# Moving the shifted taps of two channel pairs from VectorE to TensorE in a selective-scan block

## The chip, the cores and the metric

The kernel runs on one core of a Trainium2 chip. A core has five engines, each with a queue of its own that is worked in order: TensorE (PE: matrix products and transposes, into PSUM), VectorE (DVE), ScalarE (ACT), GpSimd (POOL) and SyncE (SP, which here only issues DMAs). They meet through semaphores. The metric is the device time of one execution in microseconds.

## The reference

Two sequences of 2048 rows of 512 channels go through an adaptive layer norm, a Mamba mixer with a residual, a second adaptive norm and a mixing product with a residual. All is float32. What the change touches, cut short:

```python
h = layernorm(x) * (1 + ca) + sa
h, gate = split(h @ in_proj.T)                       # 1024 channels each
h = silu(causal_conv(h, conv_w, K=4) + conv_b)       # depthwise, 4 taps
dt, B, C = split(h @ x_proj.T)                       # 128, 16, 16
dt = softplus(dt @ dt_proj.T + dt_b)
dA = exp(dt[..., None] * A)                          # 16 states per channel
dBu = (dt * h)[..., None] * B
s_t = s_(t-1) * dA_t + dBu_t
y = sum_n(s * C) + h * D
x = x + ga * ((y * silu(gate)) @ out_proj.T)
x = x + gb * (mix(layernorm(x) * (1 + cb) + sb))     # 8 factors, summed beforehand
```

## The kernel before

The rows are cut into 16 chunks of 256 (8 for each sequence). The 1024 channels are 8 tiles of 128, taken as 4 *pairs* q = 0 to 3. A *unit* is one pair with one of the 16 states: one 128x512 operation (two tiles of 256 rows side by side). A chunk has 64 units; two units are a *step* s (32 in a chunk), four units a *quad* g (16 in a chunk, four to a pair).

For each unit ScalarE makes the decay exp(dt A) in one of three PSUM banks (`decays`), VectorE scans it with `ub` = u B (`scan`), and the state is multiplied with C. VectorE does that product for most units itself (`multiply_c`, into a ring of four `sc_d`); for the others its scan writes to `state_p`, and GpSimd multiplies one or two units of a quad at once (`multiply_c` of GpSimd, into slots of `sc_p`). How many of a quad's four units are GpSimd's is in the tables `FIRST_POOL` (chunk 0), `FOLD_POOL` (chunk 1) and `EVERY_POOL` (from chunk 2): the last ones of the quad, or the first ones where the quad closes its pair (g = 3, 7, 11, 15). TensorE sums over the states by transposing each product into `y_bank` (`turn_on_dve`, `turn_on_pool`). GpSimd also makes u = dt h (`make_u`) and ub for a quad at a time (`make_ub`, two quads ahead), and the small operations that carry the state over a chunk's border (`carry_seam`, `add_column`; ScalarE's `make_column`, `add_seam`).

Beside this inner loop, chunk c's steps hold the front part of chunk c + 1 (norm, input projection, convolution, SiLU, dt, B, C) and the back part of chunk c - 1 (gate, output projection, residual, second norm, mixing). Every engine has this order written out by hand in its `one_round(c, par, la, lc)`: a call stands under the step s (or quad g) in which it is issued. There is no planner; tables such as `IN_AT`, `TAP_AT`, `ADD_AT`, `SILU_AT` give steps for the four pairs or eight tiles, the first of two entries for chunk 0, the second for the later chunks.

The convolution of pair q goes so. TensorE projects (`project_h`, in the steps of `IN_AT`) into a PSUM bank. ScalarE's `copy_h` (`TAP_AT`) copies the bank to `pre` in SBUF with three rows of the chunk before ahead of it, and scales the bank by the unshifted tap and adds the bias. VectorE's `taps` (`TAP_AT`) adds the first shifted tap to the bank, one 128x256 operation for each of the two tiles. TensorE's `add_tap` (`ADD_AT`) adds the other two as products with diagonal matrices `tap_diag`, which GpSimd made at the start. Then come ScalarE's tanh (`tanh_before`, `SILU_AT`) and VectorE's `silu_before`, which writes `hc`. For chunk 0 VectorE does all shifted taps. In `taps` the wait stands ahead of the loop:

```python
dve.wait_ge(pre_made, PAIRS * c + q + 1)
for k in range(dve_taps(c)):
```

Within one step VectorE's order is: first scan, statistics or shifts, second scan, its C products, `silu_gate`, `gate_sums`, `residual_mixer`, `silu_before`, `taps`. A norm takes variance and mean on VectorE (`stats`, `means`), the power on GpSimd (`deviations`, two operations), and -mean/deviation on VectorE (`shifts`, one 128x1 operation for each of the two row tiles).

`U_PAIRS` is the ring of u (three pairs), `DT_PAIRS` that of dt (five). `slot_table` hands out the four slots of `sc_p` in the order of the table, and `quad_before` gives the last quad that used one of a quad's slots; GpSimd's product waits until TensorE has turned it, VectorE's scan until GpSimd has multiplied it.

Of the kernel before, what the change touches and what calls it, by code (L numbers as in the profile page):

```python
# [22 lines left out]
ALU = mybir.AluOpType  # L23
ACT = mybir.ActivationFunctionType

P = 128
# [17 lines left out]
DVE_TAPS = 1  # L44
PE_TAPS = range(DVE_TAPS, TAPS - 1)
# [3 lines left out]
IN_AT = ((2, 3, 4, 5, 7, 8, 9, 10), (1, 3, 4, 5, 8, 9, 10, 11))  # L49
TAP_AT = ({5: 0, 7: 1, 10: 2, 12: 3}, {5: 0, 7: 1, 11: 2, 13: 3})  # L50
# [3 lines left out]
U_PAIRS = 3  # L54
H_TILES, Z_TILES = 3, 3
DT_PAIRS = 5
EVERY_POOL = (2, 2, 1, 1, 2, 2, 1, 2, 2, 2, 2, 1, 2, 2, 1, 1)
# [14 lines left out]
NORMS = 2 + LB  # L72
# [15 lines left out]
def dve_taps(c):  # L88
    return DVE_TAPS if c else TAPS - 1


def tap_start(c, q):

    return 2 * (PAIRS * c + q) * DVE_TAPS + 2 * (TAPS - 1 - DVE_TAPS) * (PAIRS if c else q)
# [98 lines left out]
def build(nc, x, win_m, xp_t, dt_t, wo_t, chan, cond_t, wmod, factors, bias, out):  # L193
# [11 lines left out]
    with ExitStack() as ctx:  # L205
# [19 lines left out]
        tap_diag = sb("tap_diag", [P, len(PE_TAPS), KE, P])  # L225
        decay_rate = sb("decay_rate", [P, KE, N])
# [316 lines left out]
        def _(pool):  # L543
# [26 lines left out]
            def make_u(c, q):  # L570

                pair, k = PAIRS * c + q, slice(2 * q, 2 * q + 2)
                pool.wait_ge(dt_made, pair + 1)
                pool.tensor_tensor(u[:, pair % U_PAIRS, :, :], dt[:, pair % DT_PAIRS, :, :], hc[:, k, :], ALU.mult).then_inc(u_made, 1)  # L574
# [86 lines left out]
            def make_diagonals():  # L661
# [3 lines left out]
                for i, k in enumerate(PE_TAPS):  # L665
                    pool.tensor_tensor(tap_diag[:, i, :, :], ident[:, :].unsqueeze(1).to_broadcast([P, KE, P]),
                                       conv[:, :, k:k + 1].to_broadcast([P, KE, P]), ALU.mult).then_inc(diag_made, 1)

# [5 lines left out]
            def one_round(c, par, la, lc):  # L674
                for g in range(QUADS):
# [15 lines left out]
                    if c % PER and g == 6:  # L691
                        add_column(c, slice(2, 4), 5)
                    multiply_c(quad)
                    if g in (0, 2, 3):
                        make_u(c, max(g, 1))
# [12 lines left out]
                    if la is not None and g == 12:  # L708
# [3 lines left out]
                    if c % PER and g == 4:  # L712
# [13 lines left out]
        def _(act):  # L726
# [254 lines left out]
            def one_round(c, par, la, lc):  # L981
                for s in range(STEPS):
# [34 lines left out]
                    if c % PER and s == 12:  # L1017
                        make_column(c, 3)
                    if lc is not None and s in (1, 3, 5):
                        tanh_gate(c - 1, {1: 1, 3: 2, 5: 3}[s])  # L1020
                    if s in (4, 6, 12):
                        skip(c, {4: 1, 6: 2, 12: 3}[s])
                    if la is not None:
# [8 lines left out]
                        if s == 22:  # L1032
# [38 lines left out]
        def _(pe):  # L1071
# [74 lines left out]
            def add_tap(c, q):  # L1146

                if c == 1 and q == 0:
                    pe.wait_ge(diag_made, len(PE_TAPS))
                pe.wait_ge(tap_done, tap_start(c, q) + 2 * DVE_TAPS)  # L1150
                for j in range(2):
                    for i, k in enumerate(PE_TAPS):
# [690 lines left out]
```

## Time and profile before

| | us |
|---|---|
| median of 3 runs | 1929.47 |
| lowest, highest | 1928.4, 1930.35 |
| the profiled execution | 1929.0 |
| its span (first to last instruction) | 1927.3 |
| busy in it: TensorE, VectorE, ScalarE, GpSimd | 1720.6, 1801.3, 1546.2, 1794.0 |
| mean granted TensorE clock, share of full speed | 0.975 |

Busy time is the time in which an engine has at least one instruction under way. Times in the rows below count from the start of the span. The profile was taken in an execution of its own, whose time stands in the table beside its span.

### The profile page before, as it was taken

The page shows a single profiled execution, that of the slowest core. Times are in us where ns is not written, and L with a number is a line of the kernel's source. Part 1 is how long each engine was busy: PE and PEld are TensorE (multiplying, and loading weights), DVE is VectorE, ACT ScalarE, POOL GpSimd, SP SyncE. Part 2 cuts the span into 40 slices and gives each one's busy share as a digit, 9 for nine tenths or more (in the row PEclk, how much of TensorE's full clock was granted, in tenths as well). Part 3 has the DMA queues.
Part 4 walks back from the last instruction along what each step waited for, and adds up shares of the span by engine and source line. Part 5 has one row for each costly group of instructions (what it writes and reads, how often), then busy time and mean ns, then how long its engine had stood idle before and what let it go on. Part 6 is the DMA issues. An engine that isn't in the chain of part 4 may idle for free. (4 is left out here: it accounts for less than half of the span.)

```text
span 1927.3 us, 29502 instructions
## 1 busy us (share of the span) xinstructions
PE 1720.6 (89%) x9176; PEld 1311.1 (68%) x9176; DVE 1801.3 (93%) x2260; ACT 1546.2 (80%) x4529; POOL 1794.0 (93%) x756
## 2 busy tenths in 40 slices
PE   7995998989899998998989899998989989899798
PEld 4664767667576766767677676766768676676664
DVE  3897999999999999999999999999999999999995
ACT  3776789798888979888787988879788897988773
POOL 1899999999999999999999999999999999999993
PEclk9897999999999999999999999999999999999899
DMA  5756514032140412304042340503213041321310
GB/s 179 258 115 157 145 51 163 24 128 82 55 143 20 152 50 100 110 23 164 23 153 66 116 148 23 165 23 137 72 72 127 34 152 35 104 78 44 111 28 33
DMA packets 72077, 186.17 MB, mean 97 GB/s; under 512 B 6896, under 2 KB 8560, under 8 KB 63984
## 3 DMA queue, kind: packets, MB, share of 16 engines
q1 hardware_dynamic: 68224, 176.94, 27.1%
q0 software_dynamic: 3696, 7.34, 2.4%
q8 instruction: 73, 1.20, 0.3%
q14 instruction: 84, 0.69, 0.1%
HBM read 172.20 MB, written 12.06 MB: 96 GB/s over the span
## 5 line engine op out<-in xcount | busy, mean ns | idle before, releaser
L604 POOL TENSOR_TENSOR ub<-u,b_all 128x2048 f32<-128x2048 f32 x255 | 1166.8, 4576 | 40.7 <-DMA b_all<-bc_scratch 40.7
L756 ACT ACTIVATE decay<-dt,decay_rate 128x256 f32<-128x256 f32 x2048 | 883.7, 465 | 20.4 <-DVE state_p L1548 1.1
L1548 DVE TENSOR_TENSOR_SCAN decay<-decay,ub 128x512 f32<-128x512 f32 x617 | 729.1, 1212 | 21.7 <-ACT decay L756 16.1
L620 POOL TENSOR_TENSOR sc_p<-state_p,c_all 128x1024 f32<-128x1024 f32 (+1 forms) x256 | 499.8, 1952 | 53.1 <-PE y_bank L1088 31.6
L1548 DVE TENSOR_TENSOR_SCAN state_p<-decay,ub 128x512 f32<-128x512 f32 x407 | 480.1, 1207 | 34.5 <-ACT decay L756 32.1
L1088 PE MATMUL y_bank<-ident,sc_d 128*128 128x128 f32 x2468 | 364.6, 279 | 103.6 <-DVE sc_d L1563 103.5
L1088 PEld LDWEIGHTS y_bank<-ident,sc_d 128*128 128x128 f32 x2468 | 289.0, 143 | 180.8 <-DVE sc_d L1563 127.4
L1563 DVE TENSOR_TENSOR sc_d<-decay,c_all 128x512 f32<-128x512 f32 x617 | 395.5, 675 | 7.4 <-PE y_bank L1088 1.7
L742 ACT ACTIVATE carry<-decay 128x2 f32<-128x2 f32 x617 | 99.8, 162 | 220.4 <-DVE sc_d L1563 219.0
L1170 PE MATMUL bank_a<-hT,win_h 128*128 128x256 f32 x992 | 236.3, 384 | 15.3 <-DVE hc L1612 7.8
L1088 PEld LDWEIGHTS y_bank<-ident,sc_p 128*128 128x128 f32 x1628 | 195.6, 145 | 65.5 <-issue 33.2
L1142 PE MATMUL bank_c<-hT,win_z 128*128 128x256 f32 x960 | 235.0, 392 | 1.9
L1088 PE MATMUL y_bank<-ident,sc_p 128*128 128x128 f32 x1628 | 219.4, 280 | 19.2 <-POOL sc_p L620 19.2
L1242 PE MATMUL bank_c<-wo,yg 128*128 128x512 f32 x480 | 221.4, 594 | 0.0
L1170 PEld LDWEIGHTS bank_a<-hT,win_h 128*128 128x128 f32 x992 | 181.9, 192 | 41.0 <-DVE hc L1612 10.4
L1142 PEld LDWEIGHTS bank_c<-hT,win_z 128*128 128x128 f32 x960 | 180.5, 196 | 27.3 <-DVE xc L1661 5.3
L1242 PEld LDWEIGHTS bank_c<-wo,yg 128*128 128x128 f32 x480 | 86.8, 191 | 73.5 <-issue 72.0
L1153 PE MATMUL bank_a<-pre_z,tap_diag 128*128 128x256 f32 x480 | 119.2, 392 | 13.7 <-DVE bank_a L1603 13.7
L1153 PEld LDWEIGHTS bank_a<-pre_z,tap_diag 128*128 128x128 f32 x480 | 91.1, 195 | 41.3 <-DVE bank_a L1603 17.3
L1286 PE MATMUL bank_c<-ffn,hT 128*128 128x512 f32 x240 | 112.9, 592 | 0.0
L574 POOL TENSOR_TENSOR u<-dt,hc 128x512 f32<-128x512 f32 x63 | 84.1, 1336 | 0.0
L857 ACT ACTIVATE y_rows<-y_bank 128x512 f32<-128x512 f32 x64 | 37.3, 582 | 56.7 <-PE y_bank L1088 49.8
(137 smaller groups left out, 1813.3 us busy)
## 6 DMA issues: line engine op xcount, KB each, us to landing
win_h<-win_m SPq DMA_DIRECT2D x128, 256.0 KB, 2.6
win_z<-win_m SPq DMA_DIRECT2D x128, 256.0 KB, 2.7
b_all<-bc_scratch SPq DMA_DIRECT2D x31, 1024.0 KB, 4.7
c_all<-bc_scratch SPq DMA_DIRECT2D x31, 1024.0 KB, 5.1
xa<-x SPq DMA_DIRECT2D x16, 512.0 KB, 5.1
xc<-x SPq DMA_DIRECT2D x16, 512.0 KB, 3.8
out<-xc SPq DMA_DIRECT2D x15, 512.0 KB, 3.7
ffn<-factors POOLq DMA_DIRECT2D x7, 1024.0 KB, 10.1
```

What stands on the lines that cost most here:

```text
L604: pool.tensor_tensor(ub[:, slot, :, :, :], u[:, (PAIRS * c + q) % U_PAIRS, :, :].unsqueeze(1).to_broadcast([P, QUAD, 2, ROWS]), b_all[:, n ...
L620: pool.tensor_tensor(sc_p[:, slot:slot + k, :, :], state_p[:, slot:slot + k, :, :], c_all[:, n:n + k, :].unsqueeze(2).to_broadcast([P, k, ...
L742: act.activation(dst, src, ACT.Copy).then_inc(carried, 1)
L756: last = act.activation(bk[:, j * ROWS:(j + 1) * ROWS], dt[:, pair % DT_PAIRS, j, :], ACT.Exp, scale=decay_rate[:, e, n:n + 1])
L1088: last = pe.matmul(y_bank[:, at:at + P], tile[:, j, t * P:(t + 1) * P], ident[:, :], start=False, stop=last_of_pair, is_transpose=True, sk ...
L1142: last = pe.matmul(dst[:, j * ROWS:(j + 1) * ROWS], tile[:, k, :], hTc[:, k, :], start=(k == 0), stop=(k == KD - 1))
L1153: last = pe.matmul(h_lane(c, q)[:, j * ROWS:(j + 1) * ROWS], tap_diag[:, i, 2 * q + j, :], pre[q % 2][:, j, k:k + ROWS], start=False, stop ...
L1170: last = pe.matmul(h_lane(c, q)[:, j * ROWS:(j + 1) * ROWS], win_h[i % H_TILES][:, k, :], hT[c % H_RING][:, k, :], start=(k == 0 and j == ...
L1242: last = pe.matmul(bank_c[t][:, :], yg[:, k, t * P:(t + 1) * P], wo[:, k, :], start=(k == 0), stop=(k == KE - 1))
L1286: last = pe.matmul(bank_c[t][:, :], hT[c % H_RING][:, k, t * P:(t + 1) * P], ffn[:, k, :], start=False, stop=(k == KD - 1), skip_group_che ...
L1548: dve.tensor_tensor_scan(dst, bk[:, :], ub[:, quad % UB_RING, i, :, :].rearrange("p j r -> p (j r)"), 0.0, ALU.mult, ALU.add).then_inc(sca ...
L1563: dve.tensor_tensor(sc_d[:, i % D_RING, :, :], bk[:, :].rearrange("p (j r) -> p j r", j=2), c_all[:, n:n + 1, :].to_broadcast([P, 2, ROWS] ...
```

## The change

For chunks from 1 on, VectorE adds no tap for pairs 0 and 1; TensorE adds all three shifted taps of these pairs, with a third diagonal for their four tiles that GpSimd makes at the start. Its `add_tap` waits for ScalarE's copy there and no longer for VectorE. The ring of u has two pairs, so `make_u` waits until the pair before the last has all its ub. One 128x2 operation makes both shifts of a norm. In `EVERY_POOL` quad 0 gives GpSimd one unit instead of two, quad 3 two instead of one. And steps are moved, on all engines but SyncE:

```diff
+T3 = 2
-IN_AT = ((2, 3, 4, 5, 7, 8, 9, 10), (1, 3, 4, 5, 8, 9, 10, 11))
-TAP_AT = ({5: 0, 7: 1, 10: 2, 12: 3}, {5: 0, 7: 1, 11: 2, 13: 3})
+IN_AT = ((2, 3, 4, 5, 7, 8, 9, 10), (1, 2, 3, 4, 8, 9, 10, 11))
+TAP_AT = ({5: 0, 7: 1, 10: 2, 12: 3}, {6: 0, 7: 1, 11: 2, 13: 3})
-U_PAIRS = 3
+U_PAIRS = 2
-EVERY_POOL = (2, 2, 1, 1, 2, 2, 1, 2, 2, 2, 2, 1, 2, 2, 1, 1)
+EVERY_POOL = (1, 2, 1, 2, 2, 2, 1, 2, 2, 2, 2, 1, 2, 2, 1, 1)
-NORMS = 2 + LB
+NORMS = 3
-def dve_taps(c):
-    return DVE_TAPS if c else TAPS - 1
+def dve_taps(c, q):
+    if c == 0:
+        return TAPS - 1
+    return 0 if q < T3 else DVE_TAPS
...
 # GpSimd
+                if pair >= U_PAIRS:
+                    pool.wait_ge(ub_made, N // QUAD * (pair - U_PAIRS + 1) - 1)
+                pool.tensor_tensor(first_diag[:, :, :], ident[:, :].unsqueeze(1).to_broadcast([P, 2 * T3, P]),
+                                   conv[:, 0:2 * T3, 0:1].to_broadcast([P, 2 * T3, P]), ALU.mult).then_inc(diag_made, 1)
+                    if g == 5:
+                        make_u(c, 3)
                     multiply_c(quad)
-                    if g in (0, 2, 3):
-                        make_u(c, max(g, 1))
+                    if g in (0, 3):
+                        make_u(c, {0: 1, 3: 2}[g])
-                    if la is not None and g == 12:
+                    if la is not None and g == 11:
                         make_u(c + 1, 0)
-                    if c % PER and g == 4:
+                    if c % PER and g == 5:
                         carry_seam(c, 1)
...
 # ScalarE
-                    if c % PER and s == 12:
+                    if c % PER and s == 14:
                         make_column(c, 3)
-                    if lc is not None and s in (1, 3, 5):
-                        tanh_gate(c - 1, {1: 1, 3: 2, 5: 3}[s])
-                    if s in (4, 6, 12):
-                        skip(c, {4: 1, 6: 2, 12: 3}[s])
+                    if lc is not None and s in (1, 3, 6):
+                        tanh_gate(c - 1, {1: 1, 3: 2, 6: 3}[s])
+                    if s in (3, 6, 14):
+                        skip(c, {3: 1, 6: 2, 14: 3}[s])
-                        if s == 22:
+                        if s == 23:
                             copy_bc(c + 1)
...
 # TensorE
-                pe.wait_ge(tap_done, tap_start(c, q) + 2 * DVE_TAPS)
+                if q < T3:
+                    pe.wait_ge(pre_made, PAIRS * c + q + 1)
+                else:
+                    pe.wait_ge(tap_done, tap_start(c, q) + 2 * DVE_TAPS)
                 for j in range(2):
+                    if q < T3:
+                        pe.matmul(h_lane(c, q)[:, j * ROWS:(j + 1) * ROWS], first_diag[:, 2 * q + j, :],
+                                  pre[q % 2][:, j, 0:ROWS], start=False, stop=False, skip_group_check=True)
-                    if lc is not None and s == 25:
+                    if lc is not None and s == 26:
                         ffn_bias(c - 1, 1)
                         project_ffn(c - 1, 1, (0,))
+                        if s == 25:
+                            expand_dt(c + 1, 2)
                         if s == 26:
-                            expand_dt(c + 1, 2)
-                        if s == 27:
                             expand_dt(c + 1, 3)
-                        for q, at in enumerate((9, 10, 11, 12)):
+                        for q, at in enumerate((9, 11, 11, 12)):
-                        for q, at in enumerate((13, 15, 15, 15)):
+                        for q, at in enumerate((13, 14, 15, 15)):
...
 # VectorE
-                for t in range(LB):
-                    dve.tensor_scalar(nrm[:, 1, t:t + 1], mv[:, t, 0:1], nrm[:, 0, t:t + 1], -1.0,
-                                      ALU.mult, ALU.mult).then_inc(normed, 1)
+                dve.scalar_tensor_tensor(out=nrm[:, 1, :], in0=mv[:, :, 0], scalar=-1.0, in1=nrm[:, 0, :],
+                                         op0=ALU.mult, op1=ALU.mult).then_inc(normed, 1)
-                for k in range(dve_taps(c)):
+                for k in range(dve_taps(c, q)):
-                        if s in (1, 3, 5):
-                            silu_gate(c - 1, {1: 1, 3: 2, 5: 3}[s])
+                        if s in (1, 3, 6):
+                            silu_gate(c - 1, {1: 1, 3: 2, 6: 3}[s])
-                        if s in (15, 17):
+                        if s in (14, 17):
                             residual_mixer(c - 1, s // 17)
```

## Rows read from the trace of the kernel before

**Rows 1.** The page's busy time, share of the span and instructions of each engine.

```profile
PE 1720.6 (89%) x9176; PEld 1311.1 (68%) x9176; DVE 1801.3 (93%) x2260; ACT 1546.2 (80%) x4529; POOL 1794.0 (93%) x756
```

**Rows 2.** Timeline of VectorE: start, length, line, operation, times, [idle before, ended by].

```profile
272.46 1.22 DVE L1548 TENSOR_TENSOR_SCAN state_p<-decay,ub 128x512 f32<-128x512 f32 x1 [0.32 <-POOL sc_p L620]
...
308.47 2.34 DVE L1548 TENSOR_TENSOR_SCAN decay<-decay,ub 128x512 f32<-128x512 f32 x2
...
879.12 2.34 DVE L1548 TENSOR_TENSOR_SCAN decay<-decay,ub 128x512 f32<-128x512 f32 x2
```

**Rows 3.** Busy time in two windows: length, engines (x), clock, DMA share, GB/s.

```profile
234.00:351.00 117.00, 105.12 (x576) 80.67 (x575) 113.22 (x142) 96.64 (x287) 116.84 (x51) 1.00 0.28 96
...
879.15:993.30 114.15, 104.60 (x583) 81.01 (x582) 111.32 (x140) 95.15 (x278) 110.70 (x45) 1.00 0.28 91
```

**Rows 4.** Waits in chunk 7: who waited for whom, us in total, times, longest.

```profile
PE y_bank L1088 <- DVE sc_d L1563: 5.5, 6, 1.6
...
POOL sc_p L620 <- PE y_bank L1088: 2.3, 2, 1.6
...
DVE state_p L1548 <- ACT decay L756: 1.5, 2, 1.2
...
POOL sc_p L620 <- DVE state_p L1548: 0.9, 1, 0.9
...
DVE decay L1548 <- ACT decay L756: 0.7, 1, 0.7
```

**Rows 5.** Timeline of VectorE: the end of chunk 6, then chunk 7.

```profile
856.68 1.22 DVE L1548 TENSOR_TENSOR_SCAN state_p<-decay,ub 128x512 f32<-128x512 f32 x1 [1.25 <-ACT decay L756]
...
861.38 2.33 DVE L1548 TENSOR_TENSOR_SCAN state_p<-decay,ub 128x512 f32<-128x512 f32 x2
...
870.33 1.22 DVE L1548 TENSOR_TENSOR_SCAN state_p<-decay,ub 128x512 f32<-128x512 f32 x1 [0.65 <-ACT decay L756]
...
887.35 1.23 DVE L1548 TENSOR_TENSOR_SCAN decay<-decay,ub 128x512 f32<-128x512 f32 x1 [0.75 <-ACT decay L756]
...
895.93 1.22 DVE L1548 TENSOR_TENSOR_SCAN decay<-decay,ub 128x512 f32<-128x512 f32 x1
...
899.35 0.87 DVE L1603 SCALAR_TENSOR_TENSOR bank_a<-pre_z,conv,bank_a 128x256 f32<-128x256 f32 x2
900.27 1.22 DVE L1548 TENSOR_TENSOR_SCAN state_p<-decay,ub 128x512 f32<-128x512 f32 x1
...
903.36 1.28 DVE L1644 TENSOR_TENSOR yg<-bank_c,yg 128x512 f32<-128x512 f32 x2
...
908.58 0.87 DVE L1603 SCALAR_TENSOR_TENSOR bank_a<-pre_z,conv,bank_a 128x256 f32<-128x256 f32 x2
909.36 2.34 DVE L1548 TENSOR_TENSOR_SCAN decay<-decay,ub 128x512 f32<-128x512 f32 x2
```

**Rows 6.** Timeline of ScalarE in chunks 6 and 7.

```profile
840.19 0.17 ACT L742 ACTIVATE carry<-decay 128x2 f32<-128x2 f32 x1 [0.60 <-DVE sc_d L1563]
...
852.83 1.57 ACT L878 ACTIVATE dt<-bank_a,ch 128x256 f32<-128x256 f32 x4
...
898.15 0.99 ACT L817 ACTIVATE bank_a<-bank_a,conv 128x256 f32<-128x256 f32 x2
```

**Rows 7.** Timeline of TensorE in chunk 7 (a float32 product is two instructions).

```profile
902.73 1.89 PE L1153 MATMUL bank_a<-pre_z,tap_diag 128*128 128x256 f32 x8
904.46 1.03 PE L1088 MATMUL y_bank<-ident,sc_p 128*128 128x128 f32 x8
...
913.53 3.72 PE L1170 MATMUL bank_a<-hT,win_h 128*128 128x256 f32 x16 [0.71 <-DVE hc L1612]
...
938.26 5.32 PE L1242 MATMUL bank_c<-wo,yg 128*128 128x512 f32 x12
```

**Rows 8.** GpSimd: its timeline in chunk 6; the page's costliest group.

```profile
860.29 1.29 POOL L574 TENSOR_TENSOR u<-dt,hc 128x512 f32<-128x512 f32 x1
...
L604 POOL TENSOR_TENSOR ub<-u,b_all 128x2048 f32<-128x2048 f32 x255 | 1166.8, 4576 | 40.7 <-DMA b_all<-bc_scratch 40.7
```

More of the change, by code:

```diff
@@ L85, in parts @@
     return unit // N, unit % N
-def dve_taps(c):
-    return DVE_TAPS if c else TAPS - 1
+def dve_taps(c, q):
+    if c == 0:
+        return TAPS - 1
+    return 0 if q < T3 else DVE_TAPS
 def tap_start(c, q):
-    return 2 * (PAIRS * c + q) * DVE_TAPS + 2 * (TAPS - 1 - DVE_TAPS) * (PAIRS if c else q)
+    return 2 * sum(dve_taps(i // PAIRS, i % PAIRS) for i in range(PAIRS * c + q))
 def quad_of(unit):
@@ L225, in build @@
         tap_diag = sb("tap_diag", [P, len(PE_TAPS), KE, P])
+        first_diag = sb("first_diag", [P, 2 * T3, P])
         decay_rate = sb("decay_rate", [P, KE, N])
@@ L1148, in add_tap @@
                 if c == 1 and q == 0:
-                    pe.wait_ge(diag_made, len(PE_TAPS))
-                pe.wait_ge(tap_done, tap_start(c, q) + 2 * DVE_TAPS)
+                    pe.wait_ge(diag_made, len(PE_TAPS) + 1)
+                if q < T3:
+                    pe.wait_ge(pre_made, PAIRS * c + q + 1)
+                else:
+                    pe.wait_ge(tap_done, tap_start(c, q) + 2 * DVE_TAPS)
                 for j in range(2):
+                    if q < T3:
+                        pe.matmul(h_lane(c, q)[:, j * ROWS:(j + 1) * ROWS], first_diag[:, 2 * q + j, :],
+                                  pre[q % 2][:, j, 0:ROWS], start=False, stop=False, skip_group_check=True)
                     for i, k in enumerate(PE_TAPS):
```

## The prediction

> **What bounds the kernel now.** The page's line of busy times [rows 1] says that two engines are full: VectorE 1801.3 us and GpSimd 1794.0 of 1927.3. A share of busy time doesn't say which of them sets the pace, so I cut out single chunks. VectorE's first scan of chunk 2 begins at 308.47, that of chunk 7 at 879.12 [rows 2]: (879.12 - 308.47)/5 = 114.13 us a chunk, and chunks 2 to 14 are thirteen of this kind. In chunk 7 VectorE has 111.3 us of work in 114.15, GpSimd 110.7, TensorE 104.6, ScalarE 95.2 [rows 3]. What each waits for decides [rows 4]. VectorE waits only for ScalarE's decays: 1.5 + 0.7 us. GpSimd waits 2.3 us for TensorE (slots of its products come free when TensorE has turned them) and 0.9 for VectorE. So in these chunks GpSimd follows, and has about 3.2 us to give; VectorE with its short waits for ScalarE sets the end, and TensorE is the third part of the chain: it waits 5.5 us for VectorE's products, but from 913.53 to beyond 938.26 + 5.32 its rows follow one another without a gap [rows 7].
>
> Chunks 0 and 1 are different. From 234 to 351 GpSimd is busy 116.84 of 117 us [rows 3], and in chunk 1 VectorE's scan at 272.46 waits for it [rows 2]. A saving on VectorE before that instant is lost there, so I count no gain before chunk 2. Chunk 15 prepares no next chunk and has no taps.
>
> **The change, part by part,** in the frame of chunk 7 (step 0 at 879.12).
>
> *The taps.* For pairs 0 and 1 VectorE no longer runs two 128x256 taps each: the step that held the first pair was 900.27 - 899.35 = 0.92 us longer, the second 909.36 - 908.58 = 0.78 [rows 5]. That is 1.70 us off VectorE. TensorE gets two more matmuls a pair. Each shows as two instructions; eight take 904.46 - 902.73 = 1.73 us [rows 7], so four more are 0.87 a pair, 1.73 a chunk.
>
> *The C product that moves.* The pool takes one unit fewer in quad 0 and one more in quad 3. VectorE's product of unit 2 is added in step 1 (0.59 from start to start, by the 0.6 that each of two takes at 903.36), and that of unit 13 goes from step 6, which had 903.36 - 900.27 = 3.09 us up to the gate products and keeps two scans, 2.25: minus 0.84. In step 2 the second scan, at 887.35, waits 0.75 us for a decay that ScalarE makes after a copy and a modulation [rows 5]; ScalarE's chain to it doesn't change, so the added 0.59 fills this wait and costs nothing. Were the wait gone it would cost 0.59.
>
> So VectorE alone would be 1.70 + 0.84 = 2.54 us earlier at step 8. Three things take part of it back.
>
> (a) ScalarE's copy for the skip of pair 1 moves from step 4 to 3, ahead of the decays of step 4, which come just in time: about 0.15, between 0 and the copy's own 0.9.
>
> (b) The gate product of pair 1 in step 6 needs TensorE's transposes that ended at 902.73. VectorE now reaches it at 895.93 + 0.15 + 2.83 (step 5 without gate and tap) + 2.25 + 0.58 + 0.6 = 902.34. TensorE, in an unbroken row since the first projection of step 1, gets the product of unit 2 earlier, 0.32 after the modulation that it waits for, and saves 0.44 in step 4: 902.6. Wait: 0.3.
>
> (c) TensorE then has 0.87 more at the head of steps 6 and 8. From 902.6: six matmuls for pair 0 (2.60), the pool's products of quad 1 (0.87), transposes (0.44), one VectorE product (0.44), transposes (0.44), six matmuls of pair 1 (2.60), three pool products (1.3), one VectorE product (0.44) end at 911.75. There it starts the projection that began at 913.53 [rows 7] after waiting 0.71 for VectorE's SiLU, now done at 911.45. So TensorE is 1.78 us earlier, VectorE 2.08.
>
> From there to step 17 TensorE's work is the same and gapless, so it stays 1.78 earlier. The first half of the mixer residual moves to step 14 and needs the projection of step 12: VectorE waits about 0.5 for it, and has it out of step 15. At step 17 the second half needs the 12 matmuls that ended near 943.58, the last link that held VectorE before (a gap of 0.2). I get 1.66 us there.
>
> *Steps 18 to 31.* ScalarE makes the soft-plus of the next chunk in steps 25 and 29; VectorE waits 1.25 and 0.65 us there [rows 5], and ScalarE, once past 840.19, ran without a wait for VectorE to the first [rows 6]. These waits move with the chunk and stay. The norm's shift, two instructions of 128x1, becomes one: 0.1 us saved, twice a chunk, both ahead of these waits. I take 0; if the waits were gone it is 0.2. The later copy of B and C (step 23) gives its store one step less; but the load behind it on SyncE waits for ub products that GpSimd makes after that, so nothing comes of it. The copy also feeds the second dt expansion of step 22, which may wait for it: bounds 0 and 0.4, ahead of a wait of TensorE for VectorE; I take 0. The other two expansions and a feed-forward matmul swap places around TensorE's wait for ScalarE's y copy; same work up to the last of it, 0. Input projections one step earlier: their weights' loads wait for the first projection, still in step 1, land in 2.6 us (median of the page) and are used in step 4; 0.
>
> *GpSimd.* Its work is the same. The ring of two makes it wait only for products that its own queue has already issued. New places to wait: the product of quad 3 now reuses quad 1's slots, turned in TensorE's step 6, behind the longer taps (0.85 by the chain in (c)); the carry column of pair 3 comes in step 14; u of the next chunk, which ran at 860.29 [rows 8], stands one quad and one ub product earlier, about when dt's first half is ready, near 853.6 (852.83 + half of 1.57, [rows 6]); and quad 13 must wait for quad 12 to be turned. Behind u there wait the ub product of quad 14 and the pool product of quad 12, and behind that VectorE's scan in step 27, with a slack of 861.38 - 860.29 = 1.1 us [rows 5, 8] that u's 1.29 uses up. I get a GpSimd chunk of 110.9 + 0.85 + 0.75 = 112.5, as short as VectorE's 114.15 - 1.66 = 112.5, and set 0.15 aside for that scan. The one new diagonal product, made once, lies in GpSimd's first wait of 40.7 us [rows 8].
>
> **Sum.** 1.66 - 0.15 = 1.5 us a chunk, 13 chunks: 19.5. The profiled execution took 1929.0 us (span 1927.3): 1929.0 - 19.5 = 1909.5. The median of the runs is 0.5 above it; I say 1910.
>
> A rule of the Trainium skill (Perfetto Trace Analysis, Identifying the Most-Contended Engine) says that matmul busy time misjudges TensorE and that its headroom is read from the share of weight loads. By the rows that share is 81.0 of 114.15 us, 71%; by the rule TensorE would be far from full, (c) would fall away, and the sum would be rival 1's. The rows from 913.53 on show no gap, so I side with them.
>
> **Rivals.**
> 1. TensorE's row of matmuls doesn't hold and GpSimd keeps up: 2.54 - 0.15 = 2.4 a chunk, 31 us: 1898. For it: TensorE waited 5.5 us a chunk for VectorE. Against: the gapless stretch, and GpSimd, which has 110.7 us of work against 111.75. 13%.
> 2. GpSimd becomes the bound. Its 3.2 us of waiting a chunk shrink only if the new waits stay under 1.6; with all four paid, 0.85 + 0.4 + 0.75 + 0.25 and 0.2 to 0.8 more, a chunk is 113.4 to 114.0. Gain 2 to 10 us, 1919 to 1927. For it: 97% busy, no wait of its own from quad 8 to quad 3. Against: its waits are for TensorE and shrink when it is late. 27%, 8 of them within 0.2%.
> 3. Slower: ScalarE's copy of pair 0 comes late. It moves from step 5 to the end of step 6, behind a tanh and two skip copies; there wait TensorE's taps and, though it has no tap left, VectorE's queue (the wait for the copy stands ahead of the empty loop), with every scan behind it. The old copy ended near 899.1, VectorE got to it at 899.35 [rows 5, 6]. New: decays of unit 13 after the scan of unit 11 (898.35) end at 899.45, tanh 0.5, skip 0.85, copy 1.7: 902.4, against TensorE at 902.6 and VectorE at 903.3. From 904.4 on the gain is gone. Were it a whole step later (3.57 us: 906.0), TensorE's projection would begin at 915.1 instead of 913.53, 1.6 us a chunk, 21 us: 1950. Against: 2 us of room. 14%.
>
> **How the numbers follow.** The forecast, 1.2 to 1.8 us a chunk (1906 to 1914), has 46%. 0.2% is 3.9 us, about what a measurement of this kernel can tell. Faster 46 + 13 + 19 = 78%, within 8%, slower 14%. The range goes from 1897, below rival 1, to 1925; above it I leave rival 3 and a few per cent of rival 2.
>
> **What would show it.** Right: a chunk of 112.5 to 112.8; VectorE's step 2 wait near 0.2; its waits in steps 25 and 29 as before; TensorE's wait before pair 1's taps gone and no gap from step 6 to 18; GpSimd waiting in quads 3 and 7. Wrong: a VectorE or TensorE wait for the copy L817 in step 6, VectorE waiting for GpSimd's products, or a chunk under 112.

## The result, and the profile after

The changed kernel takes 1959.15 us (median; 1958.29 to 1967.34) against 1929.91 for the kernel before, a ratio of 1.0163 (95% interval 1.0146 to 1.0181). It is 29 us slower where 20 us faster was forecast. The span of the profiled execution grew from 1927.3 to 1956.6 us. The page's busy times of the changed kernel, which answer to [rows 1]:

```profile
PE 1759.8 (90%) x9296; PEld 1359.8 (70%) x9296; DVE 1836.3 (94%) x2169; ACT 1548.2 (79%) x4529; POOL 1795.8 (92%) x757
```

One chunk's length, from late in chunk 6 to late in chunk 7, in a window (length, engines, granted clock, DMA share, GB/s), which answers to [rows 3], though that window began at VectorE's first scan of chunk 7:

```profile
875.88:991.49 115.61, 106.13 (x570) 83.28 (x569) 112.45 (x132) 95.97 (x283) 110.76 (x48) 0.97 0.26 87
```

VectorE executes 91 instructions fewer and is busy 35 us longer. I measure a chunk from one start of GpSimd's first operation for a first norm to the next: over the last eleven such starts 114.13 us before, (1687.83 - 410.04)/11 = 116.16 after.

The groups of VectorE by line and shape show where the time went. First after, then before (busy us, mean ns of one):

```profile
L1602 DVE SCALAR_TENSOR_TENSOR nrm_c<-mv_c,nrm_c 128x2 f32<-128x2 f32 x15 | 47.4, 3161 | 0.0
...
L1602 DVE SCALAR_TENSOR_TENSOR nrm_a<-mv_a,nrm_a 128x2 f32<-128x2 f32 x16 | 20.2, 1260 | 1.2 <-POOL nrm_a L567 1.2
```

```profile
L1586 DVE TENSOR_SCALAR nrm_a<-mv_a,nrm_a 128x1 f32<-128x1 f32 x32 | 5.1, 200 | 1.2 <-POOL nrm_a L562 1.2
...
L1586 DVE TENSOR_SCALAR nrm_c<-mv_c,nrm_c 128x1 f32<-128x1 f32 x30 | 4.6, 195 | 0.0
```

The shift, two elements a partition, has become VectorE's longest operation by the mean of one (3.16 us for the second norm; a scan takes 1.21): 67.6 us in 31 instructions, where 62 took 9.7. The timelines tell why. VectorE at the end of chunk 6, and GpSimd at the same time:

```profile
853.15 3.37 DVE L1602 SCALAR_TENSOR_TENSOR nrm_c<-mv_c,nrm_c 128x2 f32<-128x2 f32 x1
856.44 2.32 DVE L1565 TENSOR_TENSOR_SCAN state_p<-decay,ub 128x512 f32<-128x512 f32 x2
...
884.00 0.15 DVE L1602 SCALAR_TENSOR_TENSOR nrm_a<-mv_a,nrm_a 128x2 f32<-128x2 f32 x1
```

```profile
851.98 4.52 POOL L611 TENSOR_TENSOR ub<-u,b_all 128x2048 f32<-128x2048 f32 x1
857.73 2.36 POOL L627 TENSOR_TENSOR sc_p<-state_p,c_all 128x1024 f32<-128x1024 f32 x1 [1.23 <-DVE state_p L1565]
...
883.82 0.32 POOL L589 TENSOR_TENSOR carry<-carry,seam 128x64 f32<-128x64 f32 x1
884.10 4.53 POOL L611 TENSOR_TENSOR ub<-u,b_all 128x2048 f32<-128x2048 f32 x1
```

The shift that begins 1.17 us into a ub product ends at 856.52, with the product (856.50). The one that meets a short seam addition takes 0.15 and ends with it (884.15; 884.14). The first norm's shift met the C product ahead of that addition in eleven of the thirteen chunks from 302 us on, and took 1.2 to 1.6 us there. The profile books the time as VectorE's work, not as a wait. What it makes late shows in the waits of the same window of one chunk, which answer to [rows 4]:

```profile
PE bank_c L1272 <- ACT pre_z L779: 2.7, 1, 2.7
PE y_bank L1090 <- ACT y_rows L868: 2.7, 1, 2.7
ACT pre_z L779 <- DVE nrm_c L1602: 2.2, 1, 2.2
POOL u L581 <- ACT dt L889: 2.1, 1, 2.1
```

ScalarE needs the shift for the second norm, TensorE needs ScalarE's norm, and GpSimd then stands 2.1 us before u, a place where it did not wait before. The second row, TensorE's wait for ScalarE's y copy, is not the shift's: without the shift, in experiment 1, it is 2.90 us.

### The profile page after: what moved, and what is told of

Its sections match the earlier page's. It is cut to its first block and busy times, and to the rows that moved or that the text cites. A ratio compares the mean times of both kernels' runs of the same rounds, so it can differ in the third digit from the quotient of the medians.

```text
span 1956.6 us, 29730 instructions
## 1 busy us (share of the span) xinstructions
PE 1759.8 (90%) x9296; PEld 1359.8 (70%) x9296; DVE 1836.3 (94%) x2169; ACT 1548.2 (79%) x4529; POOL 1795.8 (92%) x757
## 3 DMA queue, kind: packets, MB, share of 16 engines
q8 instruction: 74, 1.21, 0.2%
## 5 line engine op out<-in xcount | busy, mean ns | idle before, releaser
L1099 PE MATMUL y_bank<-ident,sc_d 128*128 128x128 f32 x2468 | 371.6, 283 | 68.5 <-DVE sc_d L1580 68.4
L1099 PEld LDWEIGHTS y_bank<-ident,sc_d 128*128 128x128 f32 x2468 | 298.3, 146 | 151.0 <-DVE sc_d L1580 87.3
L1099 PE MATMUL y_bank<-ident,sc_p 128*128 128x128 f32 x1628 | 227.9, 285 | 26.0 <-POOL sc_p L627 25.8
L1099 PEld LDWEIGHTS y_bank<-ident,sc_p 128*128 128x128 f32 x1628 | 200.0, 148 | 73.8 <-issue 31.4
L1153 PE MATMUL bank_c<-hT,win_z 128*128 128x256 f32 x960 | 225.5, 380 | 1.6 <-DVE xc L1677 1.6
L1090 PE MATMUL y_bank<-ident,skipped 128*128 128x128 f32 x256 | 44.2, 301 | 43.0 <-ACT y_rows L868 43.0
```

Source lines behind the costliest of these rows:

```text
L1099: last = pe.matmul(y_bank[:, at:at + P], tile[:, j, t * P:(t + 1) * P], ident[:, :], start=False, stop=last_of_pair, is_transpose=True, sk ...
L1153: last = pe.matmul(dst[:, j * ROWS:(j + 1) * ROWS], tile[:, k, :], hTc[:, k, :], start=(k == 0), stop=(k == KD - 1))
```

## The experiments

Theory P: VectorE's shift, now with both tensors in SBUF, waits for the GpSimd operation under way. Rival F: the form itself is slow (its stride, its two columns). Rival M: the moved steps and the ring of two cost the time, and the long shift is a symptom. The chunk in the table is the mean of the last eleven, as above; intervals are 95%. The ratios of the experiments stand against runs of the kernel before on the same chip (medians 1928.19 to 1928.9).

| kernel | median us | ratio to before | chunk us |
|---|---|---|---|
| before | 1929.91 | 1 | 114.13 |
| changed | 1959.15 | 1.0163 [1.0146, 1.0181] | 116.16 |
| 1 changed, two shifts | 1922.05 | 0.9962 [0.9947, 0.9976] | 113.70 |
| 2 before, one shift | 1978.62 | 1.0258 [1.0244, 1.0273] | 117.64 |
| 3 mean in PSUM | 1928.84 | 0.9992 [0.9979, 1.0005] | 113.65 |
| 4 two narrow shifts | 1965.29 | 1.0193 [1.0170, 1.0217] | 116.67 |
| 5 as 1, feed-forward and expansions back | 1913.27 | 0.9916 [0.9903, 0.9930] | 112.75 |
| 6 as 1, u at quad 12 | 1923.70 | 0.9970 [0.9959, 0.9981] | 114.00 |
| 7 as 1, products shared out as before | 1916.73 | 0.9933 [0.9921, 0.9946] | 113.04 |
| 8 as 1, taps back on VectorE | 1936.25 | 1.0036 [1.0023, 1.0048] | 114.47 |
| 9 as 1, feed-forward back | 1912.03 | 0.9915 [0.9901, 0.9928] | 112.73 |
| 10 changed, ub products in halves | 1941.65 | 1.0071 [1.0056, 1.0087] | 114.38 |
| 11 before, taps and ring alone | 1921.43 | 0.9964 [0.9951, 0.9976] | 113.24 |
| 12 changed, feed-forward back | 1998.13 | 1.0362 [1.0348, 1.0376] | 119.63 |

**1. The change with the two shifts of before.**

```diff
-NORMS = 3
+NORMS = 2 + LB
-                dve.scalar_tensor_tensor(out=nrm[:, 1, :], in0=mv[:, :, 0], scalar=-1.0, in1=nrm[:, 0, :],
-                                         op0=ALU.mult, op1=ALU.mult).then_inc(normed, 1)
+                for t in range(LB):
+                    dve.tensor_scalar(nrm[:, 1, t:t + 1], mv[:, t, 0:1], nrm[:, 0, t:t + 1], -1.0,
+                                      ALU.mult, ALU.mult).then_inc(normed, 1)
```

> The changed kernel with each norm's shift made again by two 128x1 operations that read one tensor operand (mean) and take the deviation as a per-partition scalar. Theory P (a VectorE operation that reads two tensor operands from SBUF does not start until the GpSimd operation under way ends): the 3.4 us at step 21 and the 1.3 us at step 29 go, a chunk falls from some 116.3 to 112.5 to 113 us, total 1905 to 1918 us. Theory F (the 128x2 form with its stride of two is slow in itself): the same. Theory M (the time went into the moved steps, above all GpSimd's wait of 2.0 us a chunk for dt in front of u, and the long shift is only how the profile books it): little changes, 1950 to 1960 us.

37 us come back and the kernel beats the one before: with this one edit undone, the rest of the change gains. Its 1922.05 us lie above the 1905 to 1918 that P had named, though. Some 10 us of the forecast are still missing; experiments 5 to 9 look for them.

**2. The one shift alone, in the kernel before** (the same lines the other way round).

> The kernel before with one edit: the norm's shift as one 128x2 operation on two SBUF operands. Theory P: in the kernel before the shift at step 21 begins 0.8 us into a ub product of 4.5 us, so it lasts about 3.6 us instead of 0.3 and ScalarE's second norm waits for it; 13 to 14 chunks by 2.2 (if the wait for ScalarE in step 25 covers 1.2 of it) to 3.5 us: 1960 to 1980 us. Theory F: the same length at every call, also in the first call of the program, where GpSimd's operation has just begun. Theory M: 1928 to 1933 us.

This costs about 50 us by itself (1978.62 against 1928.9). The second norm's shifts, by line and shape:

```profile
L1585 DVE SCALAR_TENSOR_TENSOR nrm_c<-mv_c,nrm_c 128x2 f32<-128x2 f32 x15 | 53.3, 3551 | 0.0
```

The chunk grows by 117.64 - 114.13 = 3.5 us; the two shifts, by their means, by 3551 + 841 - 2 x 195 - 2 x 200 ns = 3.6. Nothing else was changed, so rival M is out for most of the time. The first norm's shift speaks against F in the same run: it met the short seam addition in eleven chunks of the loop and took 0.23 to 0.26 us; once it began 0.10 us into a ub product (VectorE, then GpSimd), and that chunk lasted 120.06 us against 117.2 to 117.9 of the others:

```profile
1004.57 4.42 DVE L1585 SCALAR_TENSOR_TENSOR nrm_a<-mv_a,nrm_a 128x2 f32<-128x2 f32 x1
```

```profile
1004.47 4.49 POOL L604 TENSOR_TENSOR ub<-u,b_all 128x2048 f32<-128x2048 f32 x1
```

**3. The second norm's mean read from a PSUM bank** (the first norm's shift as in the change).

```diff
+                    dve.tensor_copy(bank_c[0][:, 0:LB], mv[:, :, 0]).then_inc(mean_kept, 1)
...
-                dve.scalar_tensor_tensor(out=nrm[:, 1, :], in0=mv[:, :, 0], scalar=-1.0, in1=nrm[:, 0, :],
+                dve.scalar_tensor_tensor(out=nrm[:, 1, :], in0=bank_c[0][:, 0:LB], scalar=-1.0, in1=nrm[:, 0, :],
```

> The changed kernel, but for the second norm alone the mean is first copied to two free columns of a PSUM bank in step 18 and the one 128x2 shift reads it there, so that one operand comes from PSUM and one from SBUF. The first norm's shift stays as it is. Theory P: the second norm's shift takes 0.15 to 0.3 us whatever GpSimd does, the first norm's stays at 0.15 to 2.4 us; 1908 to 1930 us. Theory F (the form is slow): the second norm's shift stays near 3.4 us, 1955 to 1962 us. Theory M: 1950 to 1960 us.

By line and shape, then in VectorE's and GpSimd's timelines:

```profile
L1610 DVE SCALAR_TENSOR_TENSOR nrm_a<-mv_a,nrm_a 128x2 f32<-128x2 f32 x16 | 18.0, 1127 | 1.2 <-POOL nrm_a L568 1.2
...
L1610 DVE SCALAR_TENSOR_TENSOR nrm_c<-bank_c,nrm_c 128x2 f32<-128x2 f32 x15 | 2.0, 134 | 0.0
```

```profile
837.90 0.14 DVE L1610 SCALAR_TENSOR_TENSOR nrm_c<-bank_c,nrm_c 128x2 f32<-128x2 f32 x1
```

```profile
836.58 4.54 POOL L612 TENSOR_TENSOR ub<-u,b_all 128x2048 f32<-128x2048 f32 x1
```

The same operation, 1.32 us into a ub product of 4.54, takes 0.14 us when one of its operands lies in PSUM. In the same run the first norm's shift, with both in SBUF, still takes 1.1 us on the mean. The copy in PSUM has no stride any more, so this run alone does not separate P from the stride; experiment 4, which has no stride, and the 0.23 us of the strided form in experiment 2 do.

**4. Two narrow shifts in the form of the change.**

```diff
+                for t in range(LB):
+                    dve.scalar_tensor_tensor(out=nrm[:, 1, t:t + 1], in0=mv[:, t, 0:1], scalar=-1.0, in1=nrm[:, 0, t:t + 1],
+                                             op0=ALU.mult, op1=ALU.mult).then_inc(normed, 1)
```

> The changed kernel with each shift cut into two 128x1 operations of the new form, both tensor operands from SBUF, no stride left. Theory P: the first of each pair still waits for the end of GpSimd's operation, and the second follows at once or waits for the next one: 3.4 us or more at step 21, 1957 to 1990 us. Theory F (stride or width): 0.2 us each as in the kernel before, 1905 to 1918 us. Theory M: 1950 to 1960 us.

By line and shape:

```profile
L1603 DVE SCALAR_TENSOR_TENSOR nrm_c<-mv_c,nrm_c 128x1 f32<-128x1 f32 x30 | 57.0, 1937 | 0.0
```

Two of them together take no less than the one of 128x2 (2 x 1937 ns; 3161 ns): in thirteen chunks the pair took 3.5 us, to the end of the ub product under way, and in the first and the last 5.35 and 6.12, where the second of the two stood for the next GpSimd operation. Neither the width nor the stride is the cause; the two SBUF tensors are. `tensor_scalar` reads the same two tiles, but one as a scalar of each partition, and took 0.2 us on the mean in every run that used it (176 to 214 ns in the kernel before).

**10. GpSimd's ub products in halves, all else as in the change.**

```diff
-                pool.tensor_tensor(ub[:, slot, :, :, :], ...
+                for h in (0, QUAD // 2):
+                    made = pool.tensor_tensor(ub[:, slot, h:h + QUAD // 2, :, :], ...
+                made.then_inc(ub_made, 1)
```

> The changed kernel, one-operation shift and all, with each 128x2048 ub product of GpSimd issued as two of 128x1024. Theory P (the shift waits for the end of the GpSimd operation under way): the second norm's shift, 3.4 us when it begins 1.1 us after a ub product of 4.5, now waits for the end of a half of 2.3 and takes about 1.2; the longest shift is under 2.4; the chunk falls from 116.3 by 1 to 2.2 us, though GpSimd pays about 0.14 us more a ub product, 2.2 a chunk: 1930 to 1950. Rival F (the form is slow beside any busy GpSimd, or waits for a whole ub product to be complete): shifts stay near 3.2 us and GpSimd's price comes on top: 1957 to 1975.

By line and shape:

```profile
L1605 DVE SCALAR_TENSOR_TENSOR nrm_c<-mv_c,nrm_c 128x2 f32<-128x2 f32 x15 | 16.1, 1075 | 0.0
```

P forecast about 1.2 us and 1930 to 1950: 1.08 and 1941.65. The mean mixes cases: in six of the fifteen chunks the shift began 0.4 to 0.8 us into the first half product and ended with that half, not with the second (1.6 to 1.9 us); in seven it met the last 0.3 us of a C product; none took over 2.1. VectorE's price is what is left of the GpSimd operation that it meets, and shorter operations lowered it, although GpSimd now has more instructions to pay for.

**5 and 9. What was missing in experiment 1.** Its chunks are not alike: of the last eleven, eight last 112.0 to 113.1 us and three last 116.1. Theory C: at the boundary before a long chunk TensorE's clock falls, because TensorE now stands longer before the skip matmul that needs ScalarE's y copy. The change had moved the feed-forward bias and first matmuls from step 25, ahead of that wait, to step 26, behind it.

```diff
-                    if lc is not None and s == 26:
+                    if lc is not None and s == 25:
                         ffn_bias(c - 1, 1)
                         project_ffn(c - 1, 1, (0,))
-                        if s == 25:
-                            expand_dt(c + 1, 2)
                         if s == 26:
+                            expand_dt(c + 1, 2)
+                        if s == 27:
                             expand_dt(c + 1, 3)
```

Experiment 5 has both parts, 9 only the first.

> The first experiment's kernel (two shifts) with the step-26 work back where it was before the change: the feed-forward bias and first matmuls in step 25, the dt expansions of pairs 2 and 3 in steps 26 and 27. Theory C (clock): in the two-shift kernel ten chunks last 112.8 us, three last 116.1, and in just these three TensorE stands 2.90 us before the skip matmul that waits for ScalarE's y copy (1.59 before the change), and its granted clock is then 0.50 for 6 to 8 us. With 1.6 us of matmuls back in front, the wait is about 1.6 again, at most one chunk of 116 is left, and the time is 1921.4 - 3 x 3.3 = 1911.5, between 1908 and 1917. Rival R (the ring of two and GpSimd's new waits make the three long chunks, the clock only follows): they stay, 1919 to 1925. Rival L (the later expansions make GpSimd's u wait longer): no long chunk, but 0.4 us more in each, 1915 to 1919.

> The two-shift kernel with only the feed-forward bias and first matmuls back in step 25; the dt expansions stay where the change put them (steps 25 and 26). Theory C: TensorE's wait for ScalarE's y copy is at most the 1.6 us of before, its clock does not fall between 200 and 1790 us, no chunk of 116, chunks of 112.8; the start, which was 1.5 us later with the expansions back as well, is as in the two-shift kernel: 1910 to 1914. Rival: it is the expansions' order that decides, long chunks stay: 1917 to 1923.

In experiment 1: windows of a short chunk, a long one, and the stretch about the boundary (the first number after the engines' is the granted clock); then TensorE and GpSimd there:

```profile
519.11:631.97 112.86, 105.34 (x576) 82.39 (x575) 109.41 (x134) 96.53 (x287) 110.61 (x48) 0.98 0.26 90
631.97:748.08 116.11, 108.37 (x585) 84.39 (x584) 109.57 (x134) 96.90 (x287) 110.70 (x47) 0.97 0.26 87
626.00:634.00 8.00, 5.40 (x21) 4.96 (x22) 6.67 (x9) 7.61 (x25) 7.92 (x5) 0.61 0.02 7
```

```profile
628.60 1.09 PE L1090 MATMUL y_bank<-ident,skipped 128*128 128x128 f32 x4 [2.90 <-ACT y_rows L868]
```

```profile
640.53 2.36 POOL L627 TENSOR_TENSOR sc_p<-state_p,c_all 128x1024 f32<-128x1024 f32 x1 [3.10 <-PE y_bank L1099]
```

In experiment 9, the same stretch and the chunk after it, and TensorE:

```profile
631.72:744.48 112.76, 105.13 (x578) 80.99 (x577) 109.49 (x134) 96.54 (x287) 110.65 (x47) 1.00 0.26 90
626.00:634.00 8.00, 6.25 (x31) 3.99 (x30) 6.93 (x9) 7.61 (x26) 7.92 (x5) 1.00 0.00 0
```

```profile
628.33 0.63 PE L1090 MATMUL y_bank<-ident,skipped 128*128 128x128 f32 x4 [1.60 <-ACT y_rows L868]
```

With the wait at 2.90 us the granted clock was 0.61 from 626 to 634, most of it at the lower of its two levels, 1.2 GHz; TensorE was late with its transposes, and GpSimd stood 3.10 us for them, about the length by which the chunk is longer (3.3). With the wait at 1.60 the clock stayed at 2.4 GHz, and in both kernels no chunk of 116 is left. The times agree with C (1911.5 and 1910 to 1914 forecast; 1913.27 and 1912.03 measured), and 5 and 9 are the fastest versions, alike within the noise. Not settled is when the clock falls: in experiment 1 all nine waits between 468 and 1521 us were about 2.9 (25.9 us in all), yet, read in stretches of 2 us, the clock was down for about 7 us behind three of them, for about 3.5 behind two and not at all behind four. Only the chunks behind the three are long, so the wait alone costs nothing that can be seen.

**6 and 7. u back at quad 12; the C products of quads 0 and 3 as before.**

```diff
-                    if la is not None and g == 11:
+                    if la is not None and g == 12:
                         make_u(c + 1, 0)
```

```diff
-EVERY_POOL = (1, 2, 1, 2, 2, 2, 1, 2, 2, 2, 2, 1, 2, 2, 1, 1)
+EVERY_POOL = (2, 2, 1, 1, 2, 2, 1, 2, 2, 2, 2, 1, 2, 2, 1, 1)
```

> The two-shift kernel with the next chunk's first u back at quad 12. GpSimd waited 0.44 us a chunk for dt there (4.0 us in 9). Theory C: this wait goes, worth 0 to 0.44 in each of 13 chunks, and long chunks stay: 1916 to 1922. Rival R: the long chunks come from that wait and what it delays, they go: 1908 to 1914. Rival B: u is now too late for the ub products behind it, VectorE waits for ub in step 27: 1925 to 1935.

> The two-shift kernel with the C products of quads 0 and 3 shared out as before the change (two units and one for GpSimd instead of one and two). By the terms of the forecast VectorE gets 0.84 us back in step 6 and TensorE was only 0.3 behind, so 0.5 us a chunk: 1921.4 + 7 = 1928, between 1925 and 1932. Rival G (GpSimd's wait for TensorE in quad 3, 0.58 us a chunk, was what the move cost): same or faster, 1915 to 1922.

In 6 the long chunks stay (four of the last eleven) and nothing is gained, so GpSimd's wait for dt was not what was missing; its 1923.70 us lie just above the 1916 to 1922 of theory C. In 7 the short chunks are 113.1 instead of 112.8 us, so the moved product is worth 0.3 a chunk, less than the 0.5 that was expected; but no chunk of 116 came up, and the total was missed: 1916.73 lies in rival G's range. TensorE waits 2.9 us there too (25.9 us in nine), and its clock falls as well, mostly for about 3.5 us, but once for as long as in a long chunk of experiment 1 (the mean granted clock was 0.57 from 1532 to 1540, and 0.57 in experiment 1 from 1310 to 1318, ahead of a chunk of 116.10). Behind the fall GpSimd's row in experiment 7, at the place of the 3.10 us above, shows no wait, and its chunk lasts 113.15:

```profile
1542.08 2.36 POOL L627 TENSOR_TENSOR sc_p<-state_p,c_all 128x1024 f32<-128x1024 f32 x1
```

The kernels tell why. By the table of the change this product, quad 13's, takes slots that TensorE must first have turned for quad 12; by the table of before they come from quad 11. So it takes a fall of some 7 us and this slot together to make a chunk long. That this is what the fall costs was read from one such fall in experiment 7, and no experiment changed the slot alone.

**8 and 11. The taps' own worth.** In 8, `T3 = 0` in experiment 1's kernel. In 11, the kernel before with `T3 = 2`, the third diagonal, the ring of two, u of pairs 2 and 3 in quads 3 and 5, and the seam in quad 5; nothing else.

> The two-shift kernel with the taps of pairs 0 and 1 back on VectorE, all else kept. By the forecast VectorE is 1.70 us later a chunk and TensorE 1.73 lighter, 1.2 to 1.7 us a chunk: 1921.4 + 16 to 22, so 1937 to 1943. Rival S (VectorE's waits for ScalarE in steps 25 and 29, 1.9 us a chunk, take it up): 1921 to 1930. Theory C adds that a lighter TensorE waits more, so its clock falls at least as often as in three chunks.

> The kernel before with the taps of pairs 0 and 1 on TensorE, and the ring of two with the moves of u (pairs 2 and 3 in quads 3 and 5) and of the seam that it needs; two shifts, and no other step moved. Theory M (the other moves matter little): 1.70 us less on VectorE a chunk, 1.2 to 1.6 in the chunk, 1929 - 13 x 1.4 = 1911, between 1907 and 1914. Rival N (with the old order TensorE's two longer tap groups hold up VectorE's gate products): under 0.7 us a chunk, 1920 to 1927.

In 8 the chunks are 114.1 and 114.8, 1.3 to 2.0 us above the short ones of experiment 1, about what the forecast had; its 1936.25 us stand just under the range. In 11 the chunk is 113.24: taps and ring alone gain 0.9 us, nearer to rival N (under 0.7) than to M (1.2 to 1.6), and the time is N's. The moved steps and the moved product bring the rest, 0.5 us a chunk down to experiment 9's 112.73.

**12. The change with only the feed-forward back in step 25**, which differs from experiment 9 in the shift alone.

> The changed kernel, one-operation shift and all, with only the feed-forward bias and first matmuls back in step 25: it differs from the best kernel so far (1912.0) in the shift alone. Theory P and C together: the second norm's shift costs 3161 - 2 x 195 ns = 2.8 us a chunk, the first norm's 0.9 falls into VectorE's later wait for ScalarE, so 13 x 2.8 = 36 us and 1948, between 1944 and 1953; TensorE's clock, which in the changed kernel falls to 0.5 twice in most chunks, falls at most once. Rival D (the late shift itself makes TensorE wait for ScalarE and lowers the clock, wherever the feed-forward matmuls stand): 1955 to 1961.

Both theories missed: 1998.13 us. The shifts by shape, then the first norm's shift on VectorE and GpSimd's row beside it:

```profile
L1602 DVE SCALAR_TENSOR_TENSOR nrm_a<-mv_a,nrm_a 128x2 f32<-128x2 f32 x16 | 59.2, 3698 | 1.2 <-POOL nrm_a L567 1.2
...
L1602 DVE SCALAR_TENSOR_TENSOR nrm_c<-mv_c,nrm_c 128x2 f32<-128x2 f32 x15 | 46.7, 3111 | 0.0
```

```profile
657.80 4.41 DVE L1602 SCALAR_TENSOR_TENSOR nrm_a<-mv_a,nrm_a 128x2 f32<-128x2 f32 x1
```

```profile
657.40 0.33 POOL L589 TENSOR_TENSOR carry<-carry,seam 128x64 f32<-128x64 f32 x1
657.68 4.51 POOL L611 TENSOR_TENSOR ub<-u,b_all 128x2048 f32<-128x2048 f32 x1
```

At 884.00 in the changed kernel this shift began 0.18 us after the start of the seam addition and ended with it. Here it begins 0.40 after it, 0.12 us into the next ub product, and waits for all of that. With both shifts at their full price the chunk is 119.63 - 112.73 = 6.9 us above experiment 9's; the means of the shifts say 3.1 + 4.4 - 0.8 = 6.7 (4404 ns is the first norm's median). P holds for the length of the shift; what I had wrong was that its price in one order would be its price in another. How the 6.9 us divide is open, because TensorE stands behind the long shift:

```profile
663.98 1.11 PE L1099 MATMUL y_bank<-ident,sc_d 128*128 128x128 f32 x4 [5.33 <-DVE sc_d L1580]
```

Its granted clock is 0.50 from 662 to 668, and it falls for about 7 us like this in every chunk of the loop, as it did ahead of the long chunks of experiment 1. So rival D's mechanism, a late shift that makes TensorE wait and lowers the clock, takes part too, although the time missed D's range as well.

## Why the prediction was wrong

**The step that failed** is "The norm's shift, two instructions of 128x1, becomes one: 0.1 us saved, twice a chunk, both ahead of these waits. I take 0; if the waits were gone it is 0.2." I priced it by the count of instructions and gave no upper bound. No row of the kernel before could show the price: in its loop each VectorE operation on two tensors has one of them in a PSUM bank (the scans and products a decay bank, taps, gates and residuals theirs). The bound lay in [rows 3] and [rows 8]: GpSimd is busy 110.7 of 114.15 us, and its longest operation is a ub product of some 4.5 us, so a VectorE operation that must stand for GpSimd could cost from nothing to 4.5, twice a chunk. That is up to 9 us a chunk against a gain of 1.5; experiment 12 came to 6.9. With this bound the slower side would have had far more than 14%.

The Trainium skill (SBUF — State Buffer, Who interferes with whom) states it: a VectorE instruction with two SBUF inputs and a GpSimd instruction that reads SBUF exclude each other, whoever starts second stands still until the other is done, and with at most one SBUF input VectorE, outside its 2-port modes, does not contend. The runs agree where VectorE starts second: 3.2 us with two SBUF tensors, 0.13 with one in PSUM, 1.1 when GpSimd's ub products are halved. The other side, GpSimd standing for VectorE, no run here shows.

**The other steps,** read in experiment 9, which is the change without the shift and without the clock's falls. VectorE's timeline from the end of its chunk 6 into chunk 7, the rows with a wait:

```profile
852.16 1.22 DVE L1565 TENSOR_TENSOR_SCAN state_p<-decay,ub 128x512 f32<-128x512 f32 x1 [1.25 <-ACT decay L767]
857.39 2.34 DVE L1565 TENSOR_TENSOR_SCAN state_p<-decay,ub 128x512 f32<-128x512 f32 x2 [0.45 <-issue]
865.97 1.22 DVE L1565 TENSOR_TENSOR_SCAN state_p<-decay,ub 128x512 f32<-128x512 f32 x1 [0.28 <-ACT decay L767]
883.09 1.23 DVE L1565 TENSOR_TENSOR_SCAN decay<-decay,ub 128x512 f32<-128x512 f32 x1 [0.24 <-ACT decay L767]
898.40 0.69 DVE L1661 TENSOR_TENSOR yg<-bank_c,yg 128x512 f32<-128x512 f32 x1 [0.21 <-PE bank_c L1243]
899.26 2.35 DVE L1565 TENSOR_TENSOR_SCAN decay<-decay,ub 128x512 f32<-128x512 f32 x2 [0.17 <-ACT decay L767]
926.83 0.69 DVE L1668 TENSOR_TENSOR xc<-bank_c,xc 128x512 f32<-128x512 f32 x1 [0.28 <-PE bank_c L1259]
```

- The chunk: 112.5 to 112.8 forecast, 112.73 measured.
- Step 2: a wait of about 0.2 forecast, 0.24. The gate product: 0.3 forecast, 0.21. The residual in step 14: 0.5 forecast, 0.28. Step 25: 1.25 as before. Step 29: 0.28, not the 0.65 of [rows 5].
- The scan of step 27, behind u: 0.15 set aside, 0.45 measured, a wait to which the profile gives no releaser. VectorE is that much later in step 29, which is why the wait there shrank.
- TensorE's waits for VectorE before the taps are gone: 1.3 us in all in experiment 1, 13.7 before. From its row at 884.09 to the next wait ahead of 942.79 it has no gap, as said:

```profile
884.09 1.97 PE L1187 MATMUL bank_a<-hT,win_h 128*128 128x256 f32 x8 [0.60 <-issue]
...
942.79 0.66 PE L1099 MATMUL y_bank<-ident,sc_d 128*128 128x128 f32 x4 [0.49 <-DVE sc_d L1580]
```

- GpSimd waits where it was said to, in quads 3 (0.76; 0.85 forecast) and 7 (0.55; 0.75), and 0.45 before u, where I had about nothing (its timeline):

```profile
849.23 1.28 POOL L581 TENSOR_TENSOR u<-dt,hc 128x512 f32<-128x512 f32 x1 [0.45 <-ACT dt L889]
902.12 2.37 POOL L627 TENSOR_TENSOR sc_p<-state_p,c_all 128x1024 f32<-128x1024 f32 x1 [0.76 <-PE y_bank L1099]
932.07 2.35 POOL L627 TENSOR_TENSOR sc_p<-state_p,c_all 128x1024 f32<-128x1024 f32 x1 [0.55 <-PE y_bank L1099]
```

Two smaller steps failed besides. "The other two expansions and a feed-forward matmul swap places around TensorE's wait for ScalarE's y copy; same work up to the last of it, 0": the work was the same, the wait 1.3 us longer, and the falls of the clock behind it cost 1922.05 - 1912.03 = 10 us, three chunks by 3.3 each. And the start, where I counted neither gain nor loss, lost 2.1 us (GpSimd's first norm operation for chunk 3 at 294.88 instead of 292.75). Its cause is open: with u at quad 12 (experiment 6) the same operation starts at 293.38, but with u in quad 11 and the taps back (experiment 8) at 292.92, and with u at quad 12 and the taps alone (experiment 11) at 295.44.

**The rivals.** The first (2.4 us a chunk) did not come: TensorE's row held, although its weight loads filled only 81.0 of 112.76 us (72%) in experiment 9. The second did not decide: GpSimd's three waits are 1.8 us of its 112.76. GpSimd's wait in quad 13 for quad 12 to be turned does not show in experiment 9; in experiment 1 it is the one that carried the falls of the clock into the chunk, with 3.10 us at 640.53. The third did not come either: in chunk 7 of the changed kernel no wait for ScalarE's copy stands in step 6. The slower result came by a mechanism that was no rival.

**The sum.** Between the spans of the changed kernel and experiment 9 lie 1956.6 - 1911.0 = 45.6 us: 11 x (116.16 - 112.73) = 37.7 in the eleven chunks and 7.9 ahead of and behind them. The causes are the shift (37 us of the medians, by experiment 1) and the falls of the clock (10, by experiment 9). These shares hold for this order of undoing them: with the feed-forward matmuls put back first the kernel gets 39 us slower (experiment 12), and taking the shift out then gains 86. With both out, the rest of the change gains 16.3 us of span, where 19.5 were forecast: 1.40 a chunk instead of 1.5, and the loss at the start.

## What to carry to other kernels

Before two VectorE instructions are merged into one, look where its tensors lie: an operation that takes two tensors from SBUF can stand for the whole of a GpSimd operation under way, however small it is, so beside a busy GpSimd keep one operand in PSUM or pass it as a scalar of each partition. An operation whose price the trace cannot show gets the longest row that it can meet as its bound, not zero. And before matmuls are moved from in front of a wait to behind it, see what TensorE does in that wait.

## What the runs showed of the hardware that was not expected

- One instruction of two elements a partition took 0.14 to 4.4 us (144 ns shortest in the changed kernel, 4415 longest in experiment 12), by where it met GpSimd's row; 0.2 us of difference in its start decided over 4 us.
- The profile counts that standing as busy time of VectorE, so neither the list of waits nor the idle times name GpSimd; the mean of a tiny operation in the list by shape does.
- The granted clock of TensorE fell to the lower level within a loop that keeps it over 90% busy: in experiment 1 behind some waits of 2.9 us, and in the kernel before, eight times between 400 and 1700 us, six of them behind a wait of 1.98 us for VectorE's product (at 643.92, say, with 0.50 from 646 to 648), without a longer chunk. In experiment 9, where no wait is above 1.6 us between 306 and 1790 us, it did not fall.
